# Last stage of a fused FFN, attention, FFN kernel: the masked bias is added to the masked f on GpSimd, one VectorE instruction per ready row block instead of two

## The reference

```
x = x + 0.5 * ffn(layernorm(x))
x = x + attn(layernorm(x))
x = x + 0.5 * ffn(layernorm(x))

ffn(input):
  dots = softmax(input @ centroids.T / 0.1)
  hits = dots > 0.01
  query_sel = any(hits, axis=1)            # one flag for each row
  cluster_sel = any(hits, axis=0)          # one flag for each of 64 clusters, over ALL rows
  row_sel = cluster_sel[assignments]       # one flag for each output column
  out = where(query_sel & row_sel, input @ weight.T + bias, 0)
```

## Time and profile before

| | before |
|---|---|
| median of 3 runs | 1197.38 us (1194.45 to 1198.16) |
| the profiled execution | 1195.54 us, span 1193.6 us |
| TensorE busy over the span | 99% |
| VectorE | 67% |
| GpSimd | 37% |
| granted TensorE clock, mean | 0.998 |

### The profile page before, as it was taken

The page is one execution under the profiler, slowest core; times in us unless marked ns, Lnnn a source line. Parts: engine busy times, 40 slices in busy tenths (PEclk is TensorE's granted clock), DMA queues, the critical chain, the costliest instruction groups (busy, mean ns, idle before and its releaser), DMA issues.

```text
span 1193.6 us, 24911 instructions
## 1 busy us (share of the span) xinstructions
PE 1177.7 (99%) x10032; PEld 998.5 (84%) x10032; DVE 795.8 (67%) x1267; ACT 488.8 (41%) x708; POOL 443.5 (37%) x582
## 2 busy tenths in 40 slices
PE   7999999999999999999999999999999999999997
PEld 7888888888888888888888888888888888888886
DVE  6654554455445477787777877778777774198897
ACT  5322233222211355656656656565565663100210
POOL 1335445543424643433434334344343201050332
PEclk9999999999999999999999999999999999999999
DMA  8568776776665366566576766766655565139785
GB/s 275 157 193 225 214 207 192 218 219 181 165 176 171 98 169 169 148 169 148 159 184 156 214 172 187 195 167 170 162 141 163 127 173 195 36 126 344 278 308 195
DMA packets 363986, 219.21 MB, mean 184 GB/s; under 512 B 289760, under 2 KB 327392, under 8 KB 363872
## 3 DMA queue, kind: packets, MB, share of 16 engines
q1 hardware_dynamic: 348704, 198.22, 59.2%
q10 hardware_dynamic: 15168, 19.40, 4.7%
HBM read 123.73 MB, written 93.85 MB: 182 GB/s over the span
## 4 chain that ended last, share of the span: by engine, by line
PE 82%; DVE 6%; DMA 5%; issue 3%; SPq 2%; POOL 1%; ACT 1%; POOLq 0%; DVEq 0%
PE ps_b L289 8%; PE ps_b L291 8%; PE ps_b L290 8%; PE ps_a L289 7%; PE ps_a L291 7%; PE ps_a L290 7%; PE ps_q L291 7%; PE ps_q L289 7%; PE ps_q L290 7%; PE ps_t L296 5%; PE ps_q L1477 3%; DMA late<-x_scratch 2%; PE ps_q L303 2%; PE ps_q L305 2%; PE ps_q L1452 2%
## 5 line engine op out<-in xcount | busy, mean ns | idle before, releaser
L322 POOL TENSOR_TENSOR var_eps<-moments,eps 128x1 f32<-128x1 f32 x96 | 18.2, 190 | 390.4 <-DVE moments L318 390.4
L289 PE MATMUL ps_a<-w_hi,odd_hi 128*128 128x512 f32 x368 | 147.5, 401 | 0.0
L291 PE MATMUL ps_a<-w_hi,odd_lo 128*128 128x512 f32 x368 | 143.8, 391 | 0.0
L290 PE MATMUL ps_a<-w_lo,odd_hi 128*128 128x512 f32 x368 | 143.2, 389 | 0.0
L656 POOL TENSOR_SCALAR f_out<-f_out,token_on 128x1024 f32<-128x1024 f32 x30 | 85.6, 2852 | 77.3 <-DVE f_out L1037 77.0
L707 POOL TENSOR_TENSOR x_ring<-x_ring,f_tmp 128x1024 f32<-128x1024 f32 x32 | 77.2, 2413 | 91.4 <-DVE best L1183 57.1
L289 PE MATMUL ps_b<-proj_hi,y_hi 128*128 128x512 f32 x256 | 103.3, 404 | 0.0
L291 PE MATMUL ps_b<-proj_hi,y_lo 128*128 128x512 f32 x256 | 100.0, 391 | 0.0
L290 PE MATMUL ps_b<-proj_lo,y_hi 128*128 128x512 f32 x256 | 99.8, 390 | 0.0
L758 POOL TENSOR_TENSOR late<-late,mask 128x1024 f32<-128x1024 f32 x18 | 46.5, 2593 | 135.2 <-DMA late<-x_scratch 89.5
L331 ACT ACTIVATE y_tok<-x_ring,norms 128x1024 f32<-128x1024 f32 x64 | 79.7, 1246 | 37.9 <-ACT o_head L905 20.7
(11 more groups left out here) (218 smaller groups left out, 3088.6 us busy)
## 6 DMA issues: line engine op xcount, KB each, us to landing
xa<-in_L_attn_x SPq DMA_DIRECT2D x32, 512.0 KB, 5.0
f_tmp<-f_scratch SPq DMA_DIRECT2D x32, 512.0 KB, 4.6
x_ring<-in_L_attn_x SPq DMA_DIRECT2D x32, 512.0 KB, 3.6
f_scratch<-f_out SPq DMA_DIRECT2D x30, 512.0 KB, 3.9
x_scratch<-x_ring SPq DMA_DIRECT2D x30, 512.0 KB, 3.6
y_scratch<-xa SPq DMA_DIRECT2D x28, 512.0 KB, 4.2
ya_tok<-y_scratch SPq DMA_DIRECT2D x112, 128.0 KB, 3.3
late<-x_scratch SPq DMA_DIRECT2D x22, 512.0 KB, 6.9
```

The lines of the kernel that those rows point to most:

```text
L289: pe.matmul(acc, hi[:, k, :], w_h[:, k, cols], start=(k == 0), stop=False)
L290: pe.matmul(acc, hi[:, k, :], w_l[:, k, cols], start=False, stop=False)
L291: last = pe.matmul(acc, lo[:, k, :], w_h[:, k, cols], start=False, stop=(k == KB - 1))
```

## The change

GpSimd now issues two instructions for each ready block: f = f · mask as before, then f = f + `bias_mask`. The second waits for the first, and for block 0 also for `bias_mask`. VectorE waits for the second, and then needs one instruction, x = f · on + x, where it had two: x = bias_mask · on + x, and x = f · on + x. The semaphore between VectorE's two instructions is gone. All else is as it was.

```diff
@@ GpSimd, loop over the ready blocks k
                     f = ready_slots(k)[0]
                     pool.tensor_tensor(f[:, :], f[:, :], mask[:, :], ALU.mult).then_inc(s_masked, 1)
+                    if k == 0:
+                        pool.wait_ge(bias_masked, 1)
+                    pool.wait_ge(s_masked, 2 * k + 1)
+                    pool.tensor_tensor(f[:, :], f[:, :], bias_mask[:, :], ALU.add).then_inc(s_masked, 1)
@@ VectorE, finish_ready(k)
-                    dve.wait_ge(s_masked, k + 1)
+                    dve.wait_ge(s_masked, 2 * k + 2)
...
-                    dve.scalar_tensor_tensor(x[:, :], bias_mask[:, :], on, x[:, :], ALU.mult, ALU.add).then_inc(s_based, 1)
-                    dve.wait_ge(s_based, k + 1)
                     dve.scalar_tensor_tensor(x[:, :], f[:, :], on, x[:, :], ALU.mult, ALU.add).then_inc(s_done, 1)
```

More of the change, by code:

```diff
@@ L248, in macaron_kernel @@
         stream_in = sems("stream_in", 3)
-        s_masked, s_based, s_done = sem("s_masked"), sem("s_based"), sem("s_done")
+        s_masked, s_done = sem("s_masked"), sem("s_done")
         bias_masked = sem("bias_masked")
```

## The result

The changed kernel is slower: 1204.93 us in the median of 5 runs (1201.76 to 1205.9) against 1194.75 us (1193.13 to 1198.16) of the kernel before, a ratio of 1.007 (95% interval 1.0046 to 1.0095). The forecast was +9.5 us to 1207. What was measured depends on what is compared: the medians differ by 10.2 us, the ratio of 1.007, which is that of the means, stands for 8.4 us (5.5 to 11.4 by its interval), and the two profiled executions differ by 6.2 us (1201.76 against 1195.54); that of the changed kernel was the fastest of its runs.

A forecast was written before the change was run, and what follows sets the result against it. The end was taken to be set by the last stage's loop of store, load, GpSimd and VectorE. 6.4 + 1.1 + 6.0 + 1.1 − 5.1 = +9.5 us gave 1207 us, range 1199 to 1213.

The forecast's parts named there:

- the two engines take turns: Last stage: VectorE instructions with two SBUF inputs and GpSimd instructions reading SBUF block each other through a shared port pair.
- First part, up to block 3: Start of the last stage to VectorE's end of block 3: four instructions saved, six additions hold VectorE; +6.4 us.
- To block 7: From block 3 to block 7: an addition on the path (+2.41), one VectorE instruction less (−1.28); +1.1 us.
- the relief: Transfers in the longer stage meet less traffic, so loads and block 3's store get quicker; half of 10.2 taken, −5.1 us.
- The three passes: Loop of store, load, GpSimd and VectorE after block 7, about 22 us each time; +2.0 us each, +6.0 in all.
- the two bounds: Each addition on the other two ready blocks of a pass costs VectorE between 0 and 2.41 us; 1.1 taken.
- The last hop: From block 15 to block 17: one VectorE instruction less (−1.28), an addition more (+2.41); +1.1 us.
- The stall before the transposes: TensorE's first stall in the stage, at 1115.6 us, grows from 0.5 to several us; transposes behind it stall too.
- Waits and signs: Expected profile of the last stage: VectorE's waits for GpSimd grow from 16.5 to over 30 us, at more than four blocks.
- the row of twelve: GpSimd's first twelve instructions of the stage, 1049.7 to about 1086 us: additions of 3.4 us, multiplications of 2.6 to 3.3.
- The addition on block 17: End of the stage: GpSimd's addition on the last ready block is what VectorE's final instructions wait for.
- the link: GpSimd's addition stands between a block's load and VectorE's instruction on it, counted as +2.41 us each time on the path.

The follow-up runs named there:

- The third run: Kernel before without VectorE's bias on ready blocks; GpSimd adds unrelated data into free SBUF after its signal, nobody waits for it: ratio 1.0025.
- The fourth run: Kernel before without VectorE's bias on ready blocks; five GpSimd instructions that only write zeros come before its signal to VectorE: ratio 0.9956.
- last runs: Kernel before with GpSimd idle in the last stage and VectorE multiplying by the mask too, with four slots and with three: ratios 0.9963 and 0.9962.
- the second: Kernel before without VectorE's bias on ready blocks; GpSimd issues 17 one-column additions between its multiplication and its signal to VectorE: ratio 1.0017.

## Why the prediction was right

Right in sign and in its mechanism: the steps that it built on, that the two engines take turns and that an addition holds VectorE, are what the third, fourth and last runs showed. In size it is right against the medians (+9.5 forecast, 10.2 measured), and that is in part luck: for the profiled execution, from which its terms were taken, it said 1205.0, and the profiled execution of the changed kernel took 1201.76, so +6.2. The sizes of its terms compare as follows with that execution.

*First part, up to block 3.* Forecast 1082.6 to about 1089 (+6.4). Measured 1087.5, so +4.9. Twelve GpSimd instructions in a row lasted from 1049.91 to 1085.22; I had about 1086. I had taken 14.5 less 3.0, that is 11.5 us of holds by the six additions; in sum VectorE's instructions up to there were about 10 us longer than before.

*To block 7.* Forecast +1.1 before the relief. It was done at 1113.9 (1112.64 + 1.28) against 1110.0, so +3.9 in all, 1.0 less than at block 3. Here the loads gave back: the store of block 3 held the queue for 2.7 us (1087.53 to the load at 1090.23) instead of 5.45, and the load took 8.11 instead of 9.46 us. Between the two the queue's other transfers took 9.6 us (1090.23 to 1099.81) instead of 7.6, which the sum didn't have.

*The three passes.* Forecast +2.0 each. Between VectorE's last instructions on blocks 7, 10, 13 and 16 there were 23.28, 22.03 and 21.68 us before, and 24.22, 24.00 and 23.94 us after: +0.9, +2.0 and +2.3, together 5.2 against 6.0 less the relief in these passes. With the loads quicker by 2.1 us in the three (5.62, 5.88 and 5.52 us against 5.77, 7.72 and 5.59), the holds and the addition were dearer than taken, about 2.4 us a pass. By the rule of the Trainium skill that the prediction names (SBUF — State Buffer, "Who interferes with whom"), taken as a whole addition each time, it would have been 4.7; the truth lies at the middle of the two bounds.

*The last hop.* Forecast +1.1. From block 15's end to block 17's it was 13.8 us before and 14.3 after, +0.4; the load of block 17 took 6.0 us (1180.76 to 1186.81) instead of 8.6.

*How the terms join.* Here the sum is wrong. Its third pass ends at block 16, and its last hop begins at block 15, which VectorE does before block 16, so the two don't follow one another. VectorE's list at the end of the changed kernel, blocks 14, 15, 16 and 17 (timeline):

```profile
1169.41 3.16 DVE L1241 SCALAR_TENSOR_TENSOR late<-late,token_on 128x1024 f32<-128x1024 f32 x1
...
1179.00 1.28 DVE L1241 SCALAR_TENSOR_TENSOR late<-late,token_on 128x1024 f32<-128x1024 f32 x1
1184.80 1.28 DVE L1241 SCALAR_TENSOR_TENSOR late<-late,token_on 128x1024 f32<-128x1024 f32 x1 [4.52 <-POOL late L762]
...
1189.94 3.42 DVE L1217 SCALAR_TENSOR_TENSOR late<-k_mask,token_on,late 128x1024 f32<-128x1024 f32 x1
1193.29 1.27 DVE L1241 SCALAR_TENSOR_TENSOR late<-late,token_on 128x1024 f32<-128x1024 f32 x1
```

The last instructions on blocks 14 and 16 in the kernel before:

```profile
1162.42 1.28 DVE L1239 SCALAR_TENSOR_TENSOR late<-late,token_on 128x1024 f32<-128x1024 f32 x1
...
1175.71 1.28 DVE L1239 SCALAR_TENSOR_TENSOR late<-late,token_on 128x1024 f32<-128x1024 f32 x1
```

Blocks 14 and 16 are 8.9 us (end at 1172.57 against 1163.70) and 9.1 us later than before, but block 15, on which the last load hangs, ends only 5.8 us later (1180.28 against 1174.48). Before, two instructions stood on block 15 and the second was held (3.05 us); now there is one, of 1.28. Along the path that counts the profiled difference is +4.9 (block 3) − 1.0 (block 7) + 0.9 (block 10) + 2.0 (block 13) − 1.0 (block 15) + 0.4 (block 17) = 6.2 us. The forecast had +2.0 for the third pass where this path has −1.0.

*The relief.* Taken as 5.1; the five loads and the store gave back 8.7 us. VectorE no longer waited for block 17, so not all of the 2.5 us of its load was on the path. The relief was undersized, and so were the holds in the passes that it offset; the first part was oversized.

*TensorE.* The stall before the transposes was forecast to grow to several us, and grew from 0.5 to 5.2 us. Two points were wrong. Transposes behind it do not stall; once TensorE was late by 5 us, the later ones had room again. And TensorE lost more than it waited: its last half product starts 6.5 us later (1186.50 against 1179.98), 4.8 of it from the stall. Of the rest, 0.2 us lay there already at the start of the stage, and 1.6 go with the lower clock, below.

*Waits and signs.* Forecast over 30 us at more than four blocks, measured 25.2 us at five. In the row of twelve, additions were to take 3.4 us and took 2.66 to 3.26. The addition on block 17 was to be the last link before VectorE's final instructions. It did come last, but as a hold: it ended at 1192.28, while L1217 stood (3.42 us from 1189.94), and VectorE did not wait for block 17, where it had waited 4.75 us before.

*The weight of the link.* The sum counts the addition on the path (+2.41 each). The fourth run shows that a longer link without a hold costs nothing when VectorE's instruction is gone too. In the change itself the link isn't free: it stands in the chain that ended last. What each half of it is worth there can't be split cleanly, since a hold makes VectorE late and only then the link has no room left. The third run, with no longer signal path, costs 9 of the 14 us, by holds of somewhat different additions; the second shows that a longer link can cost nearly as much (8 us) when GpSimd is held in turn. That the changed kernel's remaining 5 us are link and hold together is inferred, not measured.

## What to carry to other kernels

Before moving an elementwise operation from VectorE to GpSimd, look at its inputs. If VectorE's neighbours have two SBUF inputs, the move frees 1.28 us of VectorE and puts 2.4 us of GpSimd work beside it that can hold it, and the better direction may be the opposite one. The sign to look for in a timeline is a VectorE instruction of 1.9 to 3.4 us where the same form takes 0.69 or 1.28 us; busy time doesn't show it, since a held instruction counts as busy.

An engine that "only waits" may still be the wrong helper: giving GpSimd nothing to do was worth 0.38% here, although VectorE then has three instructions for each ready block instead of two.

## What the runs showed of the hardware

- The hold acts on small GpSimd instructions too, from the other side: 17 one-column additions took 2.45 us beside an idle VectorE and up to 5.59 us beside a busy one.
- GpSimd instructions that only write (768 columns in 0.74 us) did not lengthen VectorE's two-input instructions.
- After TensorE had stood still for 5.24 us in the changed kernel, its granted clock was 0.66 in the mean over 1120 to 1125 us, so for part of that time it ran at the lower of its two levels (1.2 GHz). The eight transposes took 1.94 instead of 1.06 us, and from their start to the next product's second half passed 7.97 us (1120.50 to 1128.47) instead of 6.39 (1115.56 to 1121.95): 1.6 us on top of the wait.
